# Low parts of queries and keys: from GpSimd to VectorE, in a decoder layer on one core

## What is computed

```
q, k, v = heads(x @ Wq), heads(x @ Wk), heads(x @ Wv)        # 16 heads of 32
std  = softmax(q k^T / sqrt(32)) v
dgsa = (affinities(q) * amplitudes * affinities(k)^T, rows normalised) v
x = layernorm(x + ((1 - blend) * std + blend * dgsa) @ Wo)
x = layernorm(x + ssm(ctx, gate=x))     # state = state * exp(d*A) + (d*u)*B ;  y = state . C
x = layernorm(x + ffn(x))
```

## Time and profile before

| | us |
|---|---|
| median of 3 runs (1604.98 to 1620.33) | 1607.84 |
| the profiled execution | 1618.21 |
| its span, first to last instruction | 1616.0 |
| TensorE busy, matmuls | 1224.5 (76%) |
| VectorE busy | 1214.8 (75%) |
| ScalarE busy | 744.4 (46%) |
| GpSimd busy | 257.9 (16%) |
| mean granted clock of TensorE, share of full | 0.846 |

### The profile page before, as it was taken

The page is one execution under the profiler, slowest core; times in us unless marked ns, Lnnn a source line. Parts: engine busy times, 40 slices in busy tenths (PEclk is TensorE's granted clock), DMA queues, the critical chain, the costliest instruction groups (busy, mean ns, idle before and its releaser), DMA issues.

```text
span 1616.0 us, 14035 instructions
## 1 busy us (share of the span) xinstructions
PE 1224.5 (76%) x4597; PEld 573.4 (35%) x4602; DVE 1214.8 (75%) x1425; ACT 744.4 (46%) x1102; POOL 257.9 (16%) x299
## 2 busy tenths in 40 slices
PE   5664747777788857788888867778888867786895
PEld 4332212323444422233444422223444422232453
DVE  5968979789648986889547986889648985889423
ACT  6674425443376424444365524444376423443231
POOL 1000222001112221001112231001112221011111
PEclk8766978879899978789799978789799977889798
DMA  6853894655249793555259694555258694455253
GB/s 199 268 165 99 187 217 110 128 118 116 81 119 216 167 225 108 121 114 130 54 132 221 144 220 117 113 121 127 57 134 204 154 216 115 99 127 114 61 141 97
DMA packets 116759, 228.54 MB, mean 141 GB/s; under 512 B 14560, under 2 KB 25312, under 8 KB 116688
## 3 DMA queue, kind: packets, MB, share of 16 engines
q1 hardware_dynamic: 89248, 144.95, 31.6%
q0 software_dynamic: 26496, 81.80, 26.7%
q10 hardware_dynamic: 944, 0.92, 0.2%
HBM read 116.08 MB, written 29.62 MB: 90 GB/s over the span
## 4 chain that ended last, share of the span: by engine, by line
DVE 31%; PE 31%; DMA 14%; issue 7%; ACT 4%; SPq 2%; POOL 1%; DVEq 0%; ACTq 0%; POOLq 0%
PE ps L1420 12%; DVE ST L844 10%; PE ps L1390 6%; DMA qk_parts<-PT 5%; DVE ST L836 5%; DVE MX L900 4%; PE ps L1228 4%; DMA GU<-gu_tiles 4%; PE ps L1245 3%; DVE ST L847 3%; DVE BST L880 2%; DMA KS<-qk_parts 2%; DMA YA<-ST 2%; SPq L343 2%; PE ps L1334 1%
## 5 line engine op out<-in xcount | busy, mean ns | idle before, releaser
L844 DVE TENSOR_TENSOR_SCAN ST<-dA,ST 128x1024 f32<-128x1024 f32 x128 | 316.6, 2473 | 15.3 <-ACT dA L546 11.8
L1420 PE MATMUL ps<-V,GU 128*128 128x512 f16 x1024 | 251.3, 403 | 25.0 <-DMA GU<-gu_tiles 19.4
L1228 PE MATMUL ps<-KS,QS 96*128 96x512 f32 x256 | 135.8, 610 | 149.5 <-DVE MX L900 80.4
L900 DVE TENSOR_REDUCE MX<-ps 128x1 f32<-128x512 f32 x256 | 164.9, 686 | 107.0 <-PE ps L1228 107.0
L447 POOL DMA_DIRECT2D YA<-ST x128 | 109.6, 856 | 819.6 <-DVE ST L847 793.6
L546 ACT ACTIVATE dA<-DL,Aneg 128x511 f32<-128x511 f32 x256 | 168.8, 713 | 95.5 <-DVE ST L844 95.3
L677 ACT ACTIVATE PT<-ps 128x1024 f32<-128x1024 f32 x128 | 125.0, 1019 | 118.7 <-PE ps L1334 118.0
L836 DVE TENSOR_TENSOR ST<-DU,BC 128x1024 f32<-128x1024 f32 x128 | 155.9, 1218 | 12.7 <-DMA BC<-bc_rows 7.9
L847 DVE TENSOR_TENSOR ST<-ST,BC 128x1024 f32<-128x1024 f32 x128 | 159.4, 1245 | 4.4
L1420 PEld LDWEIGHTS ps<-V,GU 128*128 128x128 bf16 x1024 | 100.3, 103 | 169.7 <-issue 42.3
L1390 PE MATMUL ps<-WP,QS 128*128 128x512 f32 x512 | 145.6, 429 | 14.2 <-DVE QS L1033 13.0
(11 more groups left out here) (224 smaller groups left out, 1627.8 us busy)
## 6 DMA issues: line engine op xcount, KB each, us to landing
YA<-ST POOLq DMA_DIRECT2D x128, 512.0 KB, 7.3
BC<-bc_rows SPq DMA_DIRECT2D x64, 512.0 KB, 5.6
qk_parts<-PT SPq DMA_DIRECT2D x64, 256.0 KB, 6.6
GU<-gu_tiles SPq DMA_DIRECT2D x64, 256.0 KB, 3.5
WP<-proj_tiles SPq DMA_DIRECT2D x64, 256.0 KB, 2.8
QS<-qk_parts SPq DMA_DIRECT2D x48, 256.0 KB, 5.3
KS<-qk_parts SPq DMA_DIRECT2D x48, 256.0 KB, 6.0
RD<-PT POOLq DMA_DIRECT2D x28, 256.0 KB, 4.9
```

What stands on the lines that cost most here:

```text
L844: nc.vector.tensor_tensor_scan(flat, dA[:, a, :, :].rearrange("p e s -> p (e s)"), flat, 0.0, ALU.mult, ALU.add).then_inc(s_scan, 1)
L900: nc.vector.tensor_reduce(MX[:, j % 2, qt, h:h + 1], ps[:, n % 2, :], AX_X, ALU.max).then_inc(s_mx, 1)
L1228: mm(ps[:, n % 2, :], QS[i][0:3 * D, h, qt * P:(qt + 1) * P], KS[i][0:3 * D, h, :], start=True, stop=True).then_inc(s_xs, 1)
L1420: last = mm(ps[:, f % F_RING, :], GU[:, t % 2, k, m * P:(m + 1) * P], XHL[:, z, k, :], start=(k == 0 and z == 0), stop=(k == KT - 1 and z ...
```

## The change

The low part is made on VectorE, from the PSUM bank itself and the high part. For units 0 to 3 it stands between dBu and scan of the place's half; for units 4 to 7 ahead of the place's half, behind the maxima. GpSimd's low part goes, and with it ScalarE's wait for the low part of unit u - 2 (which guarded the copy that GpSimd read). TensorE waits for the low part, where it waited for the high part, before it fills a bank of a unit again and before the first maxima, since VectorE now reads the bank. SyncE's order is unchanged.

```diff
 # GpSimd, attention_phase
-                def low_part(u):
-                    pool.wait_ge(s_hi, 2 * NG * b + u + 1)
-                    if u >= 2:
-                        pool.wait_ge(s_part[u % 2], 32 * KT * b + 32 * (u // 2))
-                    nc.gpsimd.tensor_tensor(QKP[:, 2 + u % 2, :], PT[:, 0, u % 2, :], QKP[:, u % 2, :].bitcast(F32),
-                                            ALU.subtract).then_inc(s_lo, 1)
...
 # ScalarE, unit u
                     if u >= 2:
                         act.wait_ge(s_gsa, NG * b + u // 2)
-                        act.wait_ge(s_lo, 2 * NG * b + u - 1)
...
 # VectorE, attention_phase
+                def low_part(u):
+                    dve.wait_ge(s_hi, 2 * NG * b + u + 1)
+                    if u >= 2:
+                        dve.wait_ge(s_part[u % 2], 32 * KT * b + 32 * (u // 2))
+                    nc.vector.tensor_tensor(QKP[:, 2 + u % 2, :], ps[:, FILL_BANKS[2 * KT + u], :],
+                                            QKP[:, u % 2, :].bitcast(F32), ALU.subtract).then_inc(s_lo, 1)
+
-                def fill_half(r):
+                def fill_half(r, between=None):
                     for n, a in fill_halves(r, first):
-                        scan_half(b, n, a)
+                        scan_half(b, n, a, between)
...
                 for u in range(2 * NG):
                     if u >= NG:
                         max_tiles(b, 0, X_FIRST[u - NG], X_FIRST[u - NG + 1])
-                    fill_half(2 * KT + u)
+                        low_part(u)
+                        fill_half(2 * KT + u)
+                    else:
+                        fill_half(2 * KT + u, lambda: low_part(u))
...
 # TensorE, max_scores and bank_free
-                    pe.wait_ge(s_hi, 2 * NG * b + 4)
+                    pe.wait_ge(s_lo, 2 * NG * b + 4)
...
-                    pe.wait_ge(s_hi, 2 * NG * b + before[-1] - 2 * KT + 1)
+                    pe.wait_ge(s_lo, 2 * NG * b + before[-1] - 2 * KT + 1)
```

More of the change, by code:

```diff
@@ L456, in attention_phase @@
                 first = type(b) is int and b == 0
-                def low_part(u):
-                    pool.wait_ge(s_hi, 2 * NG * b + u + 1)
-                    if u >= 2:
-                        pool.wait_ge(s_part[u % 2], 32 * KT * b + 32 * (u // 2))
-                    nc.gpsimd.tensor_tensor(QKP[:, 2 + u % 2, :], PT[:, 0, u % 2, :], QKP[:, u % 2, :].bitcast(F32),
-                                            ALU.subtract).then_inc(s_lo, 1)
                 for r in range(4 * KT):
-                    if 2 * KT <= r < 3 * KT:
-                        low_part(r - 2 * KT)
                     for n, a in fill_halves(r, first):
                         add_y_behind(b, n, a)
-                    if r >= 3 * KT:
-                        low_part(r - 2 * KT)
                 for z in range(2):
```

## The result

| | before | after |
|---|---|---|
| median | 1607.61 us (6 runs, 1604.98 to 1620.33) | 1622.56 us (6 runs, 1614.99 to 1629.09) |
| ratio | | 1.0066, 95% interval 1.0036 to 1.0097 |
| the profiled execution | 1618.21 (span 1616.0) | 1614.99 (span 1613.2) |
| VectorE / GpSimd busy | 1214.8 / 257.9 | 1206.6 / 213.9 |

The changed kernel is slower, by 10.6 us by the ratio. The two profiled executions say the opposite, by 3 us: the one of before lies 10 us over its median, the one of after is the fastest of six.

The account below looks back on a forecast made before the run. No single engine was the bound: VectorE, TensorE and SyncE's stores take turns, with unit 4's landing ending the units' stage. Batch 0's +3.3 plus 3 x 0.0 gave +3 us on the 1607.84 median: 1611, range 1600 to 1625.

Parts of the forecast that it names:

- the store chain slips in every batch: Rival, chance 0.25: 3.0 us slip four times, perhaps a longer full stretch from earlier YA additions; 1617 to 1626.
- signs of being wrong: Unit 6's cast over 2 us off within its batch, low parts over 0.8 us, or VectorE waiting before unit 5's low part.
- signs of being right: Included batch 0's BC wait near 226, store to stack load under 5.5 us in batches 1 to 3, halves 5.34 apart.
- Price on VectorE: 32 low parts on VectorE at 0.61 us each, upper bound 0.69: 19.5 us added.
- Relief: VectorE's scans and place 14's product no longer stretched by GpSimd's low part: 6.6 us per batch, 26 us in all.
- New waits: VectorE's low parts waiting for casts: nothing for most units, +0.6 us at unit 6, whose product gives back 0.88.
- 3 us in a rival: Rival, the move stalls VectorE, chance 0.05: unit 5's low part waits for its cast, 3 us in three batches; 1630.
- Lateness of the store: Unit 2's low part made after the next dBu, so its store enters SyncE's queue 3.0 us later.
- Landing of unit 2: Batches 1 to 3: store lets the stack load go after 4.4 to 4.9 us, so landing slips only 0.7 to 1.2.
- Landing of unit 4: Batches 1 to 3: full DMA engines and earlier YA additions leave a slip of +0.3 us, between -1 and +3.
- Batch 0: Uncrowded queue gives nothing back: +3.0, +0.6 for unit 5's low part, +0.6 and -0.9 at place 14; +3.3 us.
- Sum: Whole kernel: +3.3 for batch 0 plus 3 x 0.0 for the others, +3 us on the median: 1611.

Follow-up runs that it names:

- narrow_pool: Kernel before with GpSimd's low part over 32 of the 512 columns, the rest left out: ratio 0.9974.
- before_again: Kernel before, unchanged, traced a second time: ratio 1.0015, trace of 1608.8 us.
- stack1 kernels: Second stack's loads and wait moved behind unit 4's stores, on the kernel before, early and the changed kernel: 0.9944, 0.9951, 0.9954.
- pool_late: Kernel before with GpSimd's low parts of units 0 to 3 behind the YA addition, not ahead of it: ratio 1.0092.
- early: Changed kernel with VectorE's low parts of units 0 to 3 one place earlier: ratio to before 1.0005.

## Why the prediction was right, and which of its steps were not

The range of 1600 to 1625 held the time, and so did "within 1%". That is owed to the width of the range, which took in two of the rivals, and not to the mechanism behind the forecast: 1611 missed by 11 us, and of the cases the rival "the store chain slips in every batch" (1617 to 1626) is what happened, if with a smaller slip, 1.1 us in batch 0 and 2.1 in the others, than the 3.0 that it named. That the time fell into its bounds is partly luck: the stage accounts for 7.5 us of it, and 3 to 6 us more lie elsewhere. Of the signs of being wrong that I had set, VectorE did wait ahead of unit 5's low part (3.08 us), and the cast of unit 6 came 1.9, 2.1 and 2.4 us later in batches 1 to 3, where the limit was 2. Of the signs of being right, two failed: the stack load followed the store by 5.9 to 6.6 us and not by under 5.5, and in batch 0 the wait for BC ended at 223.2 and not near 226.

- **Price on VectorE.** 0.61 us taken. Low parts take 684 ns, and a half with one is 5.20 us long; against 4.72 without one (563.66 to 568.38) that is 0.48 us each. Two overlaps and not one were gained: the low part starts 0.08 before dBu ends, and the scan 0.08 before the low part ends. Right to 0.13 us, on the safe side.
- **Relief.** 1.15 us per scan and 0.88 for the product of place 14: right, all are gone. That little of it reaches the end was right too (narrow_pool: 26 us less work, 4 us less time).
- **New waits.** Units 0 to 4 and 7 cost nothing: right. Unit 5 waited 3.08 us and I had put it at nothing, or at 3 us in a rival; it cost nothing all the same, since TensorE's next maxima come at 604.49 (before, 603.77 with a first cast 0.69 earlier). Unit 6: cast at 615.11, scan at 617.58, 2.47 us, against 612.29 and 614.21 before, 1.92: +0.55, and -0.88 in the product, as forecast.
- **Lateness of the store.** 3.0 us forecast, 2.6 measured (17.9 to 20.6 us behind the first cast): right.
- **Landing of unit 2.** The term that failed first. +0.7 to +1.2 taken, +2.0 measured (24.65 to 26.7, batches 1 to 3, three traces each). The store that leaves at 580.62 took 5.88 us to let the stack load go, not 4.4 to 4.9 (5.9 to 6.6 in the nine batches). I had taken batch 0's 4.42 over to the other batches. In batch 0 of after the step takes 4.33 again (below), so the number was right there and wrongly carried over.
- **Landing of unit 4.** The second. I let the rest of the slip vanish in the full DMA engines, +0.3. Measured at the cast of unit 6: +1.9, +2.1 and +2.4 (53.2 to 55.1, 53.6 to 55.7, 54.3 to 56.7 as means of three traces each). The stretch from the first stack load to the second grew from 14.0 to 16.8 us in batch 1 (588.89 to 602.85, 586.50 to 603.26), and that from the second to the cast of unit 6 shrank from 14.4 to 11.9 (602.85 to 617.28, 603.26 to 615.11). The DMA queues of these stretches tell more. Before (before_again), from the first stack load to the second (queue, packets, MB, share of 16 engines):

```profile
q1 hardware_dynamic: 1152, 2.10, 65.7%
q0 software_dynamic: 288, 1.05, 39.6%
```

and from there to the cast of unit 6:

```profile
q1 hardware_dynamic: 1650, 3.05, 75.3%
q0 software_dynamic: 236, 0.84, 29.2%
```

After, the first of the two stretches:

```profile
q1 hardware_dynamic: 1152, 2.10, 54.4%
q0 software_dynamic: 392, 1.41, 44.3%
```

and the second, in which q0 has no row, that is, no traffic:

```profile
q1 hardware_dynamic: 1561, 2.89, 94.5%
```

q0 carries GpSimd's transfers, the YA additions. In the first stretch q1 moves the same 1152 packets and 2.10 MB in both, and q0 moves 0.36 MB more after the change; in the second q0 falls from 0.84 MB to none. So YA additions moved from the second stretch into the first, as the rival said, and out of both: 7.04 MB before and 6.40 after. I had them 3 us earlier by place 12. GpSimd's row for the half of place 12, before_again (40.7 us behind the first cast, the row ahead of it is unit 5's low part):

```profile
603.52 1.27 POOL L461 TENSOR_TENSOR PT<-PT 128x512 fp32r<-128x512 f32 x1 [4.36 <-ACT PT L642]
604.74 0.88 POOL L447 DMA_DIRECT2D YA<-ST  x1
```

and after (34.8 us behind it):

```profile
594.85 0.86 POOL L447 DMA_DIRECT2D YA<-ST  x1 [4.47 <-DVE ST L835]
```

That is 5.9 us earlier, since VectorE is ahead and since the addition no longer stands behind a low part that waits for its cast.

Still 0.64 MB less took as long: 28.4 us from first stack load to cast before and 28.6 after. What I had overlooked is that the DMA engines can run empty while SyncE's queue is held by a wait. The 2 us around the second stack load (columns as in the earlier trace rows), before_again:

```profile
601.85:603.85 2.00, 0.62 (x2) 0.31 (x2) 1.93 (x3) 0.59 (x1) 0.33 (x1) 0.50 1.09 217
```

and after:

```profile
602.25:604.25 2.00, 2.00 (x5) 1.11 (x4) 0.36 (x1) 0.59 (x1) 0.00 (x0) 0.50 0.06 15
```

Before, YA additions (q0, 0.52 MB from 601.85 to 604.50) were still under way when the second stack's wait ended; after, next to nothing was, the stores of unit 4 stood behind the wait, and the DMA engines stood idle. In steps of a quarter of a microsecond, their share was under 0.3 for 1.5 to 2.5 us in all nine batches of after, and for 0 to 0.5 us in eight of the nine of before. The ninth, batch 3 of its first trace, has 1.5 us, and there the cast of unit 6 comes at 55.8 and not at 53.6 us. So the time that the fewer bytes could have given back was lost to idle DMA engines, and the first slip of 2.0 remains. With the second stack's wait moved (the three stack1 kernels) there is no such gap in batches 1 to 3. How much of the slip this gap alone is worth isn't shown.
- **Batch 0.** +3.3 forecast, +1.1 measured (74.3 to 75.4). There the wait for BC does end later behind the first cast, 40.8 and not 39.9 us (below), +0.9 and not +3.0: in this batch most of it was given back. In pool_late, whose store is later still, it ends at 38.4 us, so the store's lateness alone doesn't set it. From there to the cast of unit 6 it takes 18.4 and not 17.8 us, the +0.6 for unit 5's low part as forecast; this one is VectorE's new work and not lateness. I had the two kinds of batch the wrong way round.
- **Sum.** +3.3 + 3 x 0.0 became +1.1 + 3 x 2.1 = 7.4, which is what the stage shows (+7.5). The remaining 3 to 6 us of the ratios (10.6 and 13.2 us) lie outside the stage, in stages whose scatter is as large; their cause stays open.

Batch 0 of after, SyncE's queue, beside the earlier trace rows (first cast 182.38, there 182.94):

```profile
202.93 0.32 SPq L360 DMA_DIRECT2D qk_parts<-PT  x1
207.26 0.33 SPq L343 DMA_DIRECT2D QS<-qk_parts  x1
```

and VectorE, the dBu that waits for BC:

```profile
223.18 1.23 DVE L824 TENSOR_TENSOR ST<-DU,BC 128x1024 f32<-128x1024 f32 x1 [11.03 <-issue]
```

The store lets the stack load go after 4.33 us, as before (4.42). The instruction of VectorE that waited for BC starts 15.9 us after the first stack load (207.26 to 223.18), and there 17.5; that it is BC here too is taken from the earlier trace rows, since this row names no transfer.

## What to carry to other kernels

Work that moves from an idle engine to a busy one should be placed by when its result is needed, not by where the engine has a natural gap: 2.6 us of lateness cost more here than 6 us of relief per batch gave. Ahead of such a move, ask what stands behind its transfer in the issuing queue; a wait there that has nothing to do with the late transfer's reader (the second stack's) hands the delay on, and moving that wait behind one more store was worth more than the placement of the low part. And compare stages between traces, several of each: two whole spans had the wrong sign here.

## What the runs showed of the hardware

A late store is swallowed in part, even by a queue that is nearly full. Behind the first cast of batches 1 to 3, the store of unit 2's low part left at 15.8 (early), 17.9 (before), 20.6 (after) and 22.6 to 23.3 us (pool_late), and the stack load that waits for it at 23.75, 24.65, 26.7 and 27.2 us in the mean: some 7 us of lateness became 3.5. The step from one to the other in batch 1 was 8.2, 6.7, 5.9 and 4.0 us.

The DMA engines run empty when the next transfers stand behind a wait, however full they were just before: a share of 1.05 at 601.5 us and of 0.06 from 602.25 to 604.25 in after.

On VectorE and GpSimd, the page SBUF — State Buffer of the Trainium skill, section Who interferes with whom, says that a VectorE instruction with two SBUF inputs and a GpSimd instruction that reads SBUF exclude each other. The traces agree that they do: with GpSimd's low part gone, every scan takes 2.28 to 2.30 us. Of the kernel before, 19 scans found a low part running; each lost 0.13 or 0.14 us less than was left of it. Which of the two waits isn't told by who started first. The low parts over 512 columns and over 32 columns both start some 0.3 us ahead of a scan, beside dBu; the first makes the scan wait (3.44 us), the second waits for the scan (2.63 us, not 0.24). And one scan that had started 0.40 us ahead of a low part (581.88, batch 1 of before) took 4.12 us, while the low part took 1.56. Why, no run here shows. VectorE's own low part, one of whose inputs is in PSUM, takes 678 to 692 ns in all 32 places; since GpSimd only issues transfers then, this doesn't test the rule.
